# A routed mixture of experts whose slots fetch rows of x through inverted token lists, with seven batches' router statistics taken within the second cross attention

## The reference

```python
    x = x + _L1_xattn_ref(_layernorm(x, axis=-1), ctx_1024, ctx_1024, ...)
    x = x + _L1_ffn_ref(_layernorm(x, axis=-1), L1_ffn_router_W, L1_ffn_router_b, L1_ffn_W1, L1_ffn_b1, L1_ffn_W2, L1_ffn_b2)
...
        logits = jnp.einsum('bsd,de->bse', x.astype(jnp.float32), router_W) + router_b
        probs = jax.nn.softmax(logits, axis=-1)
        top1 = jnp.argmax(probs, axis=-1)
        mask = jax.nn.one_hot(top1, N_EXPERTS, dtype=x.dtype)
        gates = mask * probs.astype(x.dtype)
        h = jax.nn.relu(jnp.einsum('bsd,edf->besf', x, W1) + b1[:, None, :])
        y = jnp.einsum('besf,efd->besd', h, W2) + b2[:, None, :]
        out = jnp.einsum('bse,besd->bsd', gates, y)
```

## Time and profile before

| what | value |
|---|---|
| median of 3 runs | 2818.48 us (2810.91 to 2821.3) |
| the profiled execution | 2812.32 us, its span 2810.5 us |
| granted TensorE clock, mean | 0.962 |
| TensorE busy | 2571.2 us, 91% |
| VectorE busy | 1928.8 us, 69% |
| ScalarE busy | 1322.4 us, 47% |
| GpSimd busy | 1132.5 us, 40% |

### The profile page before, as it was taken

One profiled execution on the slowest core, in us unless ns is written; L12 is line 12 of the kernel. 1 busy time (PEld: TensorE's weight loads), 2 busy tenths in 40 slices (PEclk: granted clock), 3 DMA queues, 4 the chain that ended last, 5 costly groups with the idle time before them and its releaser, 6 DMA issues. The chain is left out here.

```text
span 2810.5 us, 50716 instructions
## 1 busy us (share of the span) xinstructions
PE 2571.2 (91%) x16973; PEld 1551.5 (55%) x16989; DVE 1928.8 (69%) x3654; ACT 1322.4 (47%) x2007; POOL 1132.5 (40%) x853
## 2 busy tenths in 40 slices
PE   7997899999967899999999999999889999749998
PEld 4775333333335556565656565656444444448997
DVE  5776798998778765657575756566477776665555
ACT  2433477666668643434343434333245554443333
POOL 3323433333047253535453535444454443152333
PEclk9999799999979999999999999999989999859999
DMA  5001322222111000000000000000133332246665
GB/s 171 0 0 40 78 66 62 64 72 59 32 60 46 1 2 2 1 1 1 2 1 1 1 2 1 2 1 1 52 83 86 77 84 71 55 155 229 218 214 194
DMA packets 105254, 160.71 MB, mean 57 GB/s; under 512 B 30877, under 2 KB 65704, under 8 KB 99432
## 3 DMA queue, kind: packets, MB, share of 16 engines
q1 hardware_dynamic: 100056, 148.01, 18.4%
q0 software_dynamic: 3408, 8.46, 0.8%
q10 hardware_dynamic: 1600, 1.61, 0.2%
HBM read 91.66 MB, written 14.96 MB: 38 GB/s over the span
## 5 line engine op out<-in xcount | busy, mean ns | idle before, releaser
L1647 ACT ACTIVATE self_PT<-self_ST 128x1024 f32<-128x1024 f32 x256 | 263.0, 1027 | 483.1 <-PE self_ST L1586 480.5
L1667 DVE TENSOR_REDUCE self_nmax<-self_SM 128x2 fp32r<-128x1024 f32 x256 | 313.1, 1223 | 199.1 <-PE self_SM L1569 198.5
L1735 POOL TENSOR_TENSOR self_U<-self_PT 128x1024 f32<-128x1024 f32 x64 | 153.1, 2392 | 498.5 <-ACT self_PT L1647 498.5
L496 DVE TENSOR_REDUCE cross_nmax<-cross_S 128x2 f32<-128x1024 f32 x256 | 307.5, 1219 | 47.0 <-PE cross_S L350 44.9
L1738 POOL TENSOR_TENSOR self_U<-self_U,self_PT 128x1024 f32<-128x1024 f32 x128 | 303.9, 2374 | 82.2 <-ACT self_PT L1647 80.0
L441 ACT ACTIVATE cross_PT<-cross_S 128x1024 f32<-128x1024 f32 x256 | 259.9, 1025 | 124.4 <-PE cross_S L361 124.0
L1596 PE MATMUL self_W<-self_PT,self_V 128*64 128x512 f32 x1024 | 233.8, 598 | 0.0
L1141 DVE TENSOR_REDUCE cross_nmax<-cross_S 128x4 f32<-128x1024 f32 x128 | 156.5, 1223 | 92.7 <-PE cross_S L968 91.6
L1078 ACT ACTIVATE cross_PT<-cross_S 128x1024 f32<-128x1024 f32 x128 | 131.1, 1024 | 128.0 <-PE cross_S L984 127.7
L1596 PEld LDWEIGHTS self_W<-self_PT,self_V 128*64 128x64 f32 x1024 | 67.8, 136 | 131.8 <-issue 115.6
L1569 PE MATMUL self_SM<-self_k_hi,self_q_hi 64*128 64x512 f32 x512 | 117.7, 456 | 22.9 <-DVE self_nmax L1667 20.1
(11 more groups left out here) (450 smaller groups left out, 6893.6 us busy)
## 6 DMA issues: line engine op xcount, KB each, us to landing
moe_staged<-in_L_ffn_W SPq DMA_DIRECT2D x36, 1024.0 KB
cross_ks<-cross_parts SPq DMA_DIRECT2D x384, 64.0 KB, 2.3
cross_qs<-cross_parts SPq DMA_DIRECT2D x376, 64.0 KB, 2.3
all_x<-in_L_ffn_W SPq DMA_DIRECT2D x14, 1024.0 KB
all_x<-sorted_rows SPq DMA_DIRECT2D x83, 130.0 KB, 2.2
cross_cT<-in_ctx_T SPq DMA_DIRECT2D x16, 512.0 KB, 4.6
sorted_rows<-all_spare_row SPq DMA_DIRECT2D x1, 5460.0 KB, 23.8
all_x<-in_x SPq DMA_DIRECT2D x8, 512.0 KB, 9.2
```

Of the source, the lines that this page charges most:

```text
L496: dve.tensor_reduce(nmax[:, g % 2, 0:R, n % PER_G], S[:, slot[st], :, :], AX.X, ALU.max, negate=True).then_inc(s_maxed, 1)
L1647: act.activation(PT[:, k, :, :], ST[:, :, :], ACT.Exp).then_inc(exped.sem, 1)
L1667: dve.tensor_reduce(nmax[:, i:2 * NT:NT], SM[:, :, :], AX.X, ALU.max, negate=True).then_inc(maxed.sem, 1)
L1735: pool.tensor_tensor(U[:, c % 2, :, :], PT[:, 0, :, :], PT[:, 1, :, :], ALU.add).then_inc(added.sem, 1)
```

## The change

*In the cross attention*: two new steps per batch, for batches 0 to 6. `rstat` takes the router's norm statistics of the batch just finished on VectorE, `rroot` their roots on GpSimd. `route` takes those of the last batch alone.

*In the routing*: three groups of 12, 12 and 8 tiles in place of four. Nothing is scattered. SP writes all rows of x, with rstd and shift, to `rows_mem` in HBM (three DMAs, 4.2 MB, behind the first two W2 loads). `spread` on VectorE splits a token's position into slot and lane, and writes one-hot arrays: a token's lane (128 wide), and its slot (42 wide) twice, times the token number and times the gate. `invert` on TensorE multiplies them over all tiles into one PSUM bank: for each lane and slot the token (`places`) and the gate (`gates`). `invert` of the first group stands ahead of pair 11's logits, that of the second behind the last pair. Seven of the eight low parts go to GpSimd; ScalarE's pieces are spread by the table `PIECES`. The 5.46 MB fill shrinks to one row.

*In the experts*: a slot's rows come by an indirect DMA of GpSimd from `rows_mem` by `places` (`gather`), two slots further ahead; `rest` is a copy by ScalarE (`keep`); the result is scattered by the same list. SP loads only W1.

```diff
+        at[("rstat", b, 0)] = UNITS * b + 36.20
+        at[("rroot", b, 0)] = UNITS * b + 36.40
...
+                elif kind == "rstat":
+                    dve.wait_ge(s_dve, nth_dve[("out", b, 1, 1)])
+                    if b:
+                        dve.wait_ge(s_rroot, 4 * b)
+                    for i in range(NT):
+                        dve.bn_stats(rstats[:, i, :], x_mem[:, NT + b * NT + i, :]).then_inc(s_rstat, 1)
+                    dve.wait_ge(s_rstat, 2 * NT * b + NT)
+                    for i in range(NT):
+                        dve.bn_aggr(rmv[:, i, :], rstats[:, i, :]).then_inc(s_rstat, 1)
...
+                elif kind == "rroot":
+                    of_b = x_rows[:, NT + b * NT:NT + (b + 1) * NT, :]
+                    pool.wait_ge(s_rstat, 2 * NT * (b + 1))
+                    pool.tensor_tensor(of_b[:, :, RSTD], rmv[:, :, 1], eps[:, :], ALU.add).then_inc(s_rroot, 1)
+                    pool.wait_ge(s_rroot, 4 * b + 1)
...
-GROUPS, NORMS = ((0, 4), (4, 12), (12, 22), (22, 32)), ((0, 4), (4, 12), (12, 22), (22, 32))
...
+GROUPS = ((0, 12), (12, 24), (24, 32))
+LEFT = NX - NT
+ROWS = ((0, 14), (14, LEFT), (LEFT, NX))
...
+PIECES = (0, 0, 0, 2, 2, 2, 2, 0, 0, 2, 2, 2, 2, 0, 0, 2)
+LOWS_BY_DVE = (7,)
...
+    def low_part(eng, e):
+        eng.wait_ge(s_w2_hi, FF // 2 * (e + 1))
+        eng.tensor_tensor(m.W2[:, e, :, 1, :], m.staged[:, e % 2, :, :], m.W2[:, e, :, 0, :].bitcast(F32),
+                          ALU.subtract).then_inc(m.s_w2_low[e % 2], 1)
...
+            if e == 2:
+                for first, last in ROWS:
+                    if last == NX:
+                        sp.wait_ge(s_root, 4)
+                    sp.dma_start(rows_mem[first * P:last * P, :].rearrange("(n p) c -> p n c", p=P), x_rows[:, first:last, :]).then_inc(m.s_rows, 16)
...
-        def scatter(g):
-            first, last = GROUPS[g]
-            pool.wait_ge(s_pos, g + 1)
-            for t in range(first, last):
-                pool.indirect_dma_start(out=sorted_rows, out_offset=bass.IndirectOffsetOnAxis(ap=position[:, t:t + 1], axis=0),
-                                        in_=x_rows[:, t, :], in_offset=None).then_inc(s_sc, 16)
...
-        for g in range(len(NORMS)):
-            root(g)
-        pool.wait_ge(consts["filled"], 16)
-        for g in range(G):
-            scatter(g)
...
+        for e in range(E):
+            if e not in LOWS_BY_DVE:
+                low_part(pool, e)
...
+        def spread(g):
+            first, last = GROUPS[g]
+            n = last - first
+
+            def per_slot(v):
+                return v[:, 0:n].unsqueeze(2).to_broadcast([P, n, N_SLOTS])
+
+            step(dve.tensor_scalar(tile_of[:, 0:n], row[:, 0:n], P / 2 - 0.5, 1.0 / P, ALU.subtract, ALU.mult))
+            step(dve.tensor_scalar(tile_of[:, 0:n], tile_of[:, 0:n], ROUND, None, ALU.add))
+            step(dve.tensor_scalar(tile_of[:, 0:n], tile_of[:, 0:n], ROUND, None, ALU.subtract))
+            step(dve.scalar_tensor_tensor(out=lane_of[:, 0:n], in0=tile_of[:, 0:n], scalar=-float(P), in1=row[:, 0:n], op0=ALU.mult, op1=ALU.add))
+            if g:
+                dve.wait_ge(s_inv, g)
+            for at, to in ((0, min(n, FF)), (FF, n)):
+                if at < to:
+                    step(dve.tensor_tensor(hot_lanes[at // FF][:, 0:to - at, :], lane.unsqueeze(1).to_broadcast([P, to - at, P]),
+                                           lane_of[:, at:to].unsqueeze(2).to_broadcast([P, to - at, P]), ALU.is_equal))
+            placed, gated = hot_tiles[:, 0:n, 0, :], hot_tiles[:, 0:n, 1, :]
+            step(dve.tensor_tensor(placed, slot_no.unsqueeze(1).to_broadcast([P, n, N_SLOTS]), per_slot(tile_of), ALU.is_equal))
+            step(dve.tensor_tensor(gated, placed, per_slot(gate), ALU.mult))
+            step(dve.tensor_tensor(placed, placed, token[:, first:last].unsqueeze(2).to_broadcast([P, n, N_SLOTS]), ALU.mult))
+            dve.sem_inc(s_spread, 1)
+
+        for i in range(NT):
+            dve.bn_stats(stats[:, i, :], x_rows[:, LEFT + i, 0:C]).then_inc(s_stat, 1)
...
-            if g < G - 1:
-                low_parts(g)
+            spread(g)
...
+        dve.wait_ge(s_inv, G)
+        step(dve.tensor_scalar(taken[:, :], inverse[:, 0, :], float(SPARE), None, ALU.add))
+        step(dve.tensor_copy(m.places[:, :], taken[:, :]))
+        step(dve.tensor_copy(m.gates[:, :], inverse[:, 1, :]))
+        dve.sem_inc(m.s_places, 1)
+        for e in LOWS_BY_DVE:
+            low_part(dve, e)
...
+        def invert(g):
+            first, last = GROUPS[g]
+            pe.wait_ge(s_spread, g + 1)
+            for t in range(first, last):
+                of = lanes_of(t - first)
+                done = pe.matmul(INV[:, 0:2 * N_SLOTS], of.bitcast(F32), hot_tiles[:, t - first, :, :].rearrange("p v n -> p (v n)"),
+                                 start=(t == 0), stop=(t == NX - 1), skip_group_check=True)
+            done.then_inc(s_inv, 1)
...
+            if 2 * m - 10 in firsts:
+                invert(group_of(2 * m - 10) - 1)
...
-            if i >= SPLIT_FROM:
-                high_part(i - SPLIT_FROM)
+            for piece in range(sum(PIECES[0:i]), sum(PIECES[0:i + 1])):
+                high_part(piece)
...
+    def keep(act, j):
+        act.copy(rest[:, j, :], xs[:, j, 0:C]).then_inc(s_kept, 1)
+
+    def gather(pool, n):
+        pool.indirect_dma_start(out=xs[:, n % DEEP, :], out_offset=None, in_=consts["rows_mem"],
+                                in_offset=bass.IndirectOffsetOnAxis(ap=m.places[:, n:n + 1], axis=0)).then_inc(s_loaded[n % DEEP], 16)
...
-                sp.wait_ge(s_normed, t * DEEP + (j + 1))
-                sp.dma_start(xs[:, j, :], tiles[bass.ds(following, 1), :, :].rearrange("a p c -> (a p) c")).then_inc(s_loaded[j], 16)
...
-                k = (j + DEEP - 1) % DEEP
-                sp.wait_ge(s_freed, t * DEEP + (j + DEEP))
-                sp.dma_start(rest[:, k, :], tiles[bass.ds(stored, 1), :, :].rearrange("a p c -> (a p) c")).then_inc(s_rest[k], 16)
...
+                act.wait_ge(s_y, t * DEEP + (j + 1))
+                keep(act, (j + 2) % DEEP)
...
+            if n + DEEP + 2 < SLOTS + AHEAD:
+                pool.wait_ge(s_kept, n + DEEP)
+                gather(pool, n + DEEP + 2)
...
-            sp.dma_start(sorted_rows.rearrange("(g p) c -> p g c", p=P),
-                         spare_row[:, :].unsqueeze(1).to_broadcast([P, SLOTS + AHEAD, XROW])).then_inc(s_filled, 16)
+            sp.wait_ge(s_id2, 1)
```

More of the change, by code:

```diff
@@ L746, in window_attention @@
                 at[("out", b, m, part)] = o + t + part
+    for b in range(B - 1):
+        at[("rstat", b, 0)] = UNITS * b + 36.20
+        at[("rroot", b, 0)] = UNITS * b + 36.40
     start = {("root", 0, 0): -31.40, ("htok", 0, 0): -30.93, ("root", 1, 0): -31.40, ("htok", 1, 0): -28.65,
@@ L2665 @@
 AHEAD, DEEP = 3, 3
-XROW = C + 4
-GATE, TOKEN, RSTD, SHIFT = C, C + 1, C + 2, C + 3
-GROUPS, NORMS = ((0, 4), (4, 12), (12, 22), (22, 32)), ((0, 4), (4, 12), (12, 22), (22, 32))
-SPLIT_FROM = 3
+XROW = C + 2
+RSTD, SHIFT = C, C + 1
+SPARE = B * T
+GROUPS = ((0, 12), (12, 24), (24, 32))
[3 more added lines that the diff above has]
+LOWS_BY_DVE = (7,)
 class MoeBuffers:
     def __init__(self, s, x_all, a):
-        self.s_w2_low, self.s_owned, self.s_b1 = s.sem("w2_low"), s.sem("owned"), s.sem("b1_in")
+        self.s_w2_low, self.s_owned, self.s_b1 = [s.sem(f"w2_low{n}") for n in range(2)], s.sem("owned"), s.sem("b1_in")
+        self.s_places, self.s_rows = s.sem("places"), s.sem("rows")
         self.s_w1 = [s.sem(f"w1_in{n}") for n in range(DEEP)]
@@ L2830, in step @@
             dve.wait_ge(s_d, count[0])
-        def stat(g):
-            first, last = NORMS[g]
-            for t in range(first, last):
-                dve.bn_stats(stats[:, t, :], x_rows[:, t, 0:C]).then_inc(s_stat, 1)
-            dve.wait_ge(s_stat, first + last)
-            for t in range(first, last):
-                dve.bn_aggr(mv[:, t, :], stats[:, t, :]).then_inc(s_stat, 1)
         def choose(g):
@@ L2847, in choose @@
             lg, t_0, t_1 = (v[:, 0:n, :] for v in (logit[:, g % 2, :, :], t0, t1[:, g % 2, :, :]))
-            gate = x_rows[:, first:last, GATE]
             dve.wait_ge(s_logit, last)
@@ L2896, in place @@
             step(dve.tensor_reduce(row[:, 0:n], t_0, AX.X, ALU.add))
-            step(dve.tensor_copy(position[:, first:last], row[:, 0:n]))
             dve.sem_inc(s_pos, 1)
@@ L2931, in dve_program @@
         dve.sem_inc(m.s_owned, 1)
-        for e in range(G - 1, E):
-            low_parts(e)
+        dve.wait_ge(s_inv, G)
[5 more added lines that the diff above has]
+            low_part(dve, e)
     def pe_program(pe):
@@ L2967, in count_of @@
             last.then_inc(s_cnt, 1)
-        pe.wait_ge(s_load, 64)
+        def invert(g):
[6 more added lines that the diff above has]
+            done.then_inc(s_inv, 1)
+        firsts = [first for first, _ in GROUPS[1:]]
+        pe.wait_ge(s_load, 48)
```

(22 more changed lines are left out.)

138 lines of the change are left out of this document (67 added, 71 removed).

## The result

| | before | changed |
|---|---|---|
| median | 2813.21 us (5 runs, 2810.91 to 2821.3) | 2836.23 us (5 runs, 2826.58 to 2836.74) |
| profiled execution, its span | 2812.32, 2810.5 | 2826.58, 2824.8 |
| ratio of times | 1 | 1.0059 (95%: 1.0038 to 1.0079) |

The account below looks back on a forecast made before the run. The routing's 90.8 us were taken to lie on the path in full, the loop to be TensorE work. Cross attention +2.7 and routing +8.6 gave +11.3, 2823.6 us by the profile; forecast 2826, range 2802 to 2840.

Parts of the forecast that it names:

- the sum of 8.6 us for the routing: Routing's start to first expert product: 99.4 us forecast against 90.8 before, so +8.6.
- the rival with slower batches of the cross attention (2833): Low parts take 5.4 us and cross attention batches lose 0.5 or more each: 9 more, 2833; chance 0.15.
- The stops, 26.7 us: Routing: each GpSimd low part stops VectorE until its end, 4.2 to 4.7 us; six on the path, 26.7 together.
- Parts 2 and 3 fall into the first group's spread: Routing: low parts 2 and 3 run during the first group's spread on VectorE and push it out, 4.7 us each.
- The second group: Routing: starts 52.3 us in, after the first group's 47.7, one-hot products 2.8 and logits 1.8.
- The first rows of x come at the same time: Routing's end: places 0.6, gather 1.0, landing 2.9, norm, transposes and copy 1.7 give 99.6, beside the first product's 99.4.
- The cross attention, 2.7 us: Seven batches' statistics there: six delay 0.9 us in all, the seventh 1.8 in the drain; bounds 1.8 to 12.6.
- the 5 us that I had named as the sign: A cross attention ending later by 5 us would make the forecast's first part, +2.7, wrong.
- 0.15 late each: Cross attention: six statistics of 1.8 us, ahead of maxima where VectorE idles 1.66, delay 0.15 us each, 0.9 in all.
- GpSimd has nothing due there: Cross attention: the four small roots on GpSimd delay nothing; no time was added for them.
- The loop, 0: Expert loop: the added gather and copy fit the slack of GpSimd and ScalarE, cost 0; slots stay 6.62 us apart.
- Rule and row: Routing: VectorE waits for GpSimd's whole instruction (rule, 2823.6 us) or at most 1.0 us, the longest row (2803).

Follow-up runs that it names:

- rows_later: Changed kernel with the rows' writes to HBM moved behind the W2 loads for experts 2 and 3; routing 106.0 us against 99.5, span 2844.2.
- small_low_parts: Changed kernel with every W2 low part computed for 8 elements a lane only, zero elsewhere; routing 89.3 us against 99.5, span 2822.4.
- root_behind_bias: Changed kernel with GpSimd's roots in the cross attention behind the bias addition; tenth to last `mrow` 254.5 us against 258.9, span 2829.1.

## Why the prediction came out as it did

I forecast 2826 us with a range of 2802 to 2840 and a profiled execution longer by 11.3. The direction and what a stop does were right, the time, 2836.2, lies in the range, and the sum of 8.6 us for the routing met 8.8. That agreement is in large part luck, since terms that were off cancel. The sum as a whole was too small: 18.2 us by stages in the profiled pair, nearer to the rival with slower batches of the cross attention (2833), whose other half, low parts of 5.4 us, did not come. The medians' 23.0 us hold some 5 more, for which I had no term; in the three longer runs TensorE's mean clock was 0.955 or 0.956 instead of 0.961. Term by term:

- *The stops, 26.7 us.* Measured on VectorE: 0.4, 3.9, 1.3, 3.6, 3.8, 4.0, in all 17.0. The length of a low part was right, 4.54 us (4.6 forecast), and so was what a stop does; the number of stops on the path was not. The step that failed is "Parts 2 and 3 fall into the first group's spread". I had ScalarE's pieces in the pairs 9 to 12 with their load in time, and gave the three row writes ahead of that load no term for how long they hold SP. In the changed kernel part 2 ran while VectorE was idle and part 3 cost 1.3 us. With the load in time, in rows_later, the two parts do fall into the spread, cost 4.4 and 4.3 us against 4.7 each, and the second group starts at 53.7 against the 52.3 forecast.
- *The second group.* Its start was forecast at 52.3 us and came at 46.2, set by TensorE waiting for ScalarE waiting for the load, not by the stops.
- *The end of the routing.* I had 0.6 us from the owners to the places, 1.0 for the gather's issue and 2.9 for its landing. Places and gates came 1.5 after the owners, since TensorE's last one-hot products take 3.7. The gather's issue began 1.0 after them, 0.85 us into VectorE's last low part (2536.43 to 2538.72), took 2.53 and landed 5.0 later, beside the load of W1 that SP had issued 1.4 us before it. These put back the 5.7 us that the third group's earlier end (84.7 in place of 90.4) had saved. Here the failed step is "The first rows of x come at the same time", which took the landing from a transfer of another kind. Why it lands later than the scatters' 2.9 was not taken apart; in small_low_parts, where nothing on VectorE held the issue up, it landed 5.3 after it.
- *The cross attention, 2.7 us.* Measured 9.3, past the 5 us that I had named as the sign that this part is wrong. The statistics themselves, "0.15 late each", cost 0.0 in the five batches that root_behind_bias could show undisturbed; the sentence that failed is "GpSimd has nothing due there". The bias addition was due, behind the roots in GpSimd's queue, and reached VectorE's multiplication 3.5 us later than before. I had the port's rule in hand and applied it to the routing alone. The seventh cost its 1.8 us as forecast, and TensorE's clock, which fell in five executions of six with this order, added 1.7 here, for which I had no term.
- *The loop, 0.* Right: 278.1 and 278.2.

**Rule and row.** Each of the five stops over 1 us in the routing ends 0.0 to 0.1 us after GpSimd's instruction, whatever is left of it, up to 4.1 us; waits capped at 1.0 us are refuted by the rows of L2883, L2890, L2905 and L2925. This is what the Trainium skill (SBUF — State Buffer, SBUF: two separate sides) says of the shared ports. One row is of another form than two inputs in SBUF: L2905, an addition and a multiplication by constants, has one operand in SBUF and 8 elements a lane, and took 3.97 us instead of 0.17. The same sentence of the Trainium skill counts operations in a two-port performance mode too, and no run here tells whether this one was in it.

## What to carry to other kernels

Work moved to GpSimd "beside" VectorE cost VectorE the rest of GpSimd's instruction each time VectorE's next one had two operands in SBUF. On this chain of short dependent VectorE instructions it was cheaper to do it on VectorE (91.1 against 99.5 us), and cutting it up gained 0.7 us. When a small step is put into a queue, look at what is queued behind it and at whom that meets then: here 1.8 us of small roots, waiting for their statistics, pushed a 2.2 us addition into another engine's way. And a late transfer can hide a conflict: removing the wait alone made the routing 6.4 us longer.
